# A pipelined attention step in a different order: output and value products moved between two phases of the scores

## The reference

```python
q = split_heads(xn @ Wq (+ bq)); k = split_heads(src @ Wk (+ bk)); v = split_heads(src @ Wv (+ bv))
attn = softmax(q @ k.T * scale (+ mask or relative bias))     # L3_xattn has no softmax
x = x + merge_heads(attn @ v) @ Wo (+ bo)                     # L1_xattn has no Wo; L1/L3_xattn norm afterwards
```

## Time and profile before

| | |
|---|---|
| median of 3 runs | 4896.71 us (4893.21 to 4901.27) |
| the profiled execution | 4900.09 us |
| its span, first to last instruction | 4898.2 us |
| TensorE busy | 4007.7 us, 82% |
| VectorE busy | 3203.4 us, 65% |
| GpSimd busy | 2994.6 us, 61% |
| ScalarE busy | 2059.5 us, 42% |
| mean granted TensorE clock | 0.889 |
| chains run about | 0 to 660, 1240 to 2040, 2300 to 2940, 3680 to 4690 us |

### The profile page before, as it was taken

How to read it: one execution, slowest core, us unless ns; L and a number is a source line. 1 busy time by engine, 2 the same in 40 slices (tenths; PEclk the granted TensorE clock), 3 DMA queues, 4 the chain that set the end, 5 groups by cost and what they waited for, 6 DMA issues and landing times. The chain is left out here.

```text
span 4898.2 us, 215645 instructions
## 1 busy us (share of the span) xinstructions
PE 4007.7 (82%) x85067; PEld 2918.6 (60%) x85076; DVE 3203.4 (65%) x10848; ACT 2059.5 (42%) x5737; POOL 2994.6 (61%) x4949
## 2 busy tenths in 40 slices
PE   8999977254899978656999997559879998889988
PEld 6777754132566666523777774335547776667766
DVE  5875668422344688787556874753337878888866
ACT  4555545011344444365555554112225543336632
POOL 6766632276455699688556762038876777777710
PEclk9999988555899998755999997879998999999999
DMA  3000012433100022200000002113431000000000
GB/s 94 5 13 19 19 28 57 78 62 54 37 0 0 18 39 39 35 1 1 2 0 15 22 18 54 42 46 75 77 62 35 0 15 16 16 9 1 0 13 24
DMA packets 380509, 139.58 MB, mean 28 GB/s; under 512 B 216487, under 2 KB 373239, under 8 KB 380055
## 3 DMA queue, kind: packets, MB, share of 16 engines
q1 hardware_dynamic: 345430, 107.60, 9.3%
q0 software_dynamic: 34816, 28.34, 4.0%
HBM read 91.46 MB, written 43.85 MB: 28 GB/s over the span
## 5 line engine op out<-in xcount | busy, mean ns | idle before, releaser
L1051 DVE TENSOR_REDUCE rowmax<-ps 128x16 f32<-128x1024 f32 x512 | 626.3, 1223 | 488.0 <-PE ps L678 487.7
L696 PE MATMUL ps<-prob,kT 32*64 32x256 f32 x9216 | 781.7, 408 | 8.7 <-issue 2.4
L721 PE MATMUL ps<-v,probT 64*64 64x64 f32 x36864 | 764.6, 227 | 5.3 <-issue 2.2
L721 PEld LDWEIGHTS ps<-v,probT 64*64 64x64 f32 x36864 | 683.8, 140 | 57.4 <-issue 16.0
L678 PE MATMUL ps<-kblock,qT 32*64 32x256 f32 x8192 | 697.0, 410 | 17.2 <-DVE rowmax L1060 14.2
L900 ACT ACTIVATE probT<-ps 128x1024 f32<-128x1024 f32 x512 | 518.0, 1012 | 353.4 <-PE ps L708 353.0
L585 POOL TENSOR_TENSOR kblock<-kT,key_scale 128x512 f32<-128x512 f32 x576 | 599.8, 1041 | 18.2 <-ACT kT L878 7.6
L587 POOL TENSOR_TENSOR prob<-qT,key_scale 128x512 f32<-128x512 f32 x576 | 601.5, 1044 | 0.0
L561 POOL TENSOR_TENSOR vareps<-moments,eps 128x1 f32<-128x1 f32 x522 | 98.8, 189 | 745.7 <-DVE negmean L1025 745.6
L887 ACT ACTIVATE xn<-x_res,nmr,rstd 128x128 f32 (+1 forms) x512 | 252.7, 494 | 513.6 <-POOL nmr L567 349.5
L708 PEld LDWEIGHTS ps<-mT,pick_bf 32*64 32x64 bf16 x16384 | 311.7, 108 | 221.2 <-ACT mT L857 74.1
(11 more groups left out here) (380 smaller groups left out, 9655.7 us busy)
## 6 DMA issues: line engine op xcount, KB each, us to landing
ctxT<-in_ctxT SPq DMA_DIRECT2D x256, 64.0 KB, 1.8
held<-in_g_w SPq DMA_DIRECT2D x16, 836.0 KB
ctxT<-in_ctxT SPq DMA_DIRECT2D x256, 32.0 KB, 1.9
table<-prob SPq DMA_DIRECT2D x32, 256.0 KB, 2.4
x_dram<-x_res SPq DMA_DIRECT2D x32, 256.0 KB, 2.4
x_res<-x_dram SPq DMA_DIRECT2D x16, 512.0 KB, 6.9
x_res<-in_x SPq DMA_DIRECT2D x8, 512.0 KB, 7.5
x_res<-in_e_w SPq DMA_DIRECT2D x64, 64.0 KB
```

The costliest lines, as they stand in the source:

```text
L696: mm = nc.tensor.matmul(out.rearrange("p (h s) -> p h s", h=GH), k.kT[rows, buf, S * b:S * b + S], k.qblock[rows, buf, :, S * b:S * b + S] ...
L721: mm = nc.tensor.matmul(k.ps_o[S * b:S * b + S, u, S * hh:S * hh + S], k.probT[rows, buf, at:at + S], k.v9[rows, buf, (HD + 1) * h:(HD + 1 ...
L1051: nc.vector.tensor_reduce(spread, heads, AX.X, ALU.max).then_inc(soft.did["max_raw"], 1)
```

## The change

TensorE's step starts with the q and k products. Then follow the transposition of xn, the waits of the scores (`scores_writable`, which now asks for `max_raw` and no longer for `max_done`), the transposition of the maxima, mask rows, scores phase one; then the wait for Exp of the tile to be mixed, output product, values, transposition of o; then scores phase two, with the maxima subtracted ahead of the key scores; and last the mix.

ScalarE handles the front (mT, xnT, q, k) first, then oT and v. DVE takes the maximum of the scores ahead of the mix scaling, and its two remainders behind it. The value product is one of 128 columns again (L1_xattn keeps two), and the exchange of the sequences is made by the copy or bias add out of PSUM, in three pieces. The extra columns of xnT and their copy go.

```diff
+def value_parts():
+    first, second, low, high = slice(0, HEADS // 2), slice(HEADS // 2, HEADS), slice(0, S), slice(S, P)
+    return [(slice(0, P), first, slice(0, P)), (low, second, high), (high, second, low)]
...
-        if value is not None or turn is not None or out is not None:
-            after(pe, c, values_read(c, it, 4), it, 4)
-            after(pe, c, "y_read", it, 9)
-            after(pe, c, "oT_done", it, 8)
-        if out is not None:
-            mm = nc.tensor.matmul(k.ps_y, k.oT[:, b8, :], weights(out, 3), start=True, stop=True)
...
+        if mixes is not None:
+            after(pe, c, "v_done", it, mb)
         after(pe, c, "kT_done", it, 3)
...
-            after(pe, c, "max_done", it, 4)
+            after(pe, c, "max_raw", it, 4)
             after(pe, c, "kblock_done", it, 3)
...
         if less is not None:
-            values_mixable(mixes, it, mb)
-            if early:
-                scores_writable(score1, score2, it)
+            scores_writable(score1, score2, it)
             after(pe, c, "max_done", it, 5)
...
-        if mixes is not None:
-            for hh in range(HEADS // 2):
-                mm = mix(mixes, (par - mb) % NB, hh)
-            mm.then_inc(mixes.did["o_psum"], 1)
...
             mm.then_inc(score2.did["first_rows"], 1)
 
+        mm = None
+        if mixes is not None:
+            after(pe, c, "exp_done", it, mb)
+        if value is not None or turn is not None or out is not None:
+            after(pe, c, values_read(c, it, 4), it, 4)
+            after(pe, c, "y_read", it, 9)
+            after(pe, c, "oT_done", it, 8)
+        if out is not None:
+            mm = nc.tensor.matmul(k.ps_y, k.oT[:, b8, :], weights(out, 3), start=True, stop=True)
...
+                mm = nc.tensor.matmul(k.ps_v, source[:, 0:P], wv, start=True, stop=True)
+        if turn is not None:
+            after(pe, c, "on_done", it, 7)
+            mm = nc.tensor.transpose(k.ps_oT, k.o[:, b7, :], k.ident)
+        if mm is not None:
+            mm.then_inc(c.yv_psum, 1)
+
         if score1 is not None:
             after(pe, c, "low_rows", it, 3)
             query_scores(score1, b3, high).then_inc(score1.did["s1_psum"], 1)
...
-            mm = key_scores(score2, b5, low, first=False)
             if less is not None:
                 for h in range(GH):
-                    mm = less_max(less, b5, h, low)
+                    less_max(less, b5, h, low)
+            mm = key_scores(score2, b5, low, first=False)
             mm.then_inc(score2.did["s2_psum"], 1)
+
+        if mixes is not None:
+            for hh in range(HEADS // 2):
+                mm = mix(mixes, (par - mb) % NB, hh)
+            mm.then_inc(mixes.did["o_psum"], 1)
...
-                nc.vector.tensor_tensor(values(k, b3), heads_of(k.ps_v), heads_of(bias),
-                                        ALU.add).then_inc(value.did["v_done"], 1)
+                for rows, heads, source in value_parts() if value.softmax else [WHOLE]:
+                    mm = nc.vector.tensor_tensor(values(k, b3)[rows, heads, :], heads_of(k.ps_v)[source, heads, :],
+                                                 heads_of(bias)[source, heads, :], ALU.add)
+                mm.then_inc(value.did["v_done"], 1)
...
-        k.xnT = sb("xnT", [P, NB, P + S])
+        k.xnT = sb("xnT", [P, NB, P])
```

More of the change, by code:

```diff
@@ L698, in key_scores @@
                     k.qblock[rows, buf, :, S * b:S * b + S],
-                    start=not part.softmax or first, stop=not part.softmax, tile_position=place)
+                    start=not part.softmax or first, stop=not part.softmax or groups == low, tile_position=place)
         return mm
@@ L709, in less_max @@
                     out[:, S * h:S * h + S], k.pick_bf[rows, S * h:S * h + S], k.mT[rows, buf, S * b:S * b + S],
-                    start=False, stop=groups == low and h == GH - 1, tile_position=place)
+                    start=False, stop=False, tile_position=place)
         return mm
@@ L818, in step @@
             mm.then_inc(score2.did["first_rows"], 1)
+        mm = None
[7 more added lines that the diff above has]
+            mm = nc.tensor.matmul(k.ps_y, k.oT[:, b8, :], weights(out, 3), start=True, stop=True)
+        if mixes is not None and turn is None:
+            after(pe, c, "on_done", it, mb + 1)
+        if value is not None:
+            source, wv = k.ctxT[:, b3, :] if value.cross else k.xnT[:, b3, :], weights(value, 2)
+            if value.name == "L1_xattn":
+                nc.tensor.matmul(k.ps_v[:, 0:S], source[:, 0:P], wv[:, 0:S], start=True, stop=True)
+                mm = nc.tensor.matmul(k.ps_v[:, S:P], source[:, S:S + P], wv[:, S:P], start=True, stop=True)
+            else:
+                mm = nc.tensor.matmul(k.ps_v, source[:, 0:P], wv, start=True, stop=True)
[4 more added lines that the diff above has]
+            mm.then_inc(c.yv_psum, 1)
         if score1 is not None:
@@ L842, in step @@
         plain = plain if plain is not None and plain.name == "L3_xattn" else None
[L843 to L847, removed]
-            nc.scalar.activation(k.oT[:, b7, :], k.ps_oT, ACT.Copy).then_inc(turn.did["oT_done"], 1)
-        if value is not None and value.name not in VALUE_BIAS:
-            act.wait_ge(c.yv_psum, it - 2)
-            after(act, c, "y_read", it, 8)
-            after(act, c, "o_psum", it, 3 + NB)
-            nc.scalar.activation(values(k, b3), heads_of(k.ps_v), ACT.Copy).then_inc(value.did["v_done"], 1)
         if norm is not None or project is not None or soft is not None:
@@ L864, in step @@
             else:
-                if not norm.cross:
-                    nc.scalar.activation(k.xnT[:, b1, P:P + S], k.ps_xT[:, 0:S], ACT.Copy)
                 nc.scalar.activation(k.xnT[:, b1, 0:P], k.ps_xT, ACT.Copy).then_inc(norm.did["xT_done"], 1)
@@ L878, in step @@
                 nc.scalar.activation(k.kT[:, b2, :], k.ps_k, ACT.Copy).then_inc(project.did["kT_done"], 1)
+        if turn is not None:
+            act.wait_ge(c.yv_psum, it - 2)
+            after(act, c, "y_read", it, 8)
+            if c.name(it, 3) in VALUE_BIAS:
+                after(act, c, values_read(c, it, 3), it, 3)
+            nc.scalar.activation(k.oT[:, b7, :], k.ps_oT, ACT.Copy).then_inc(turn.did["oT_done"], 1)
+        if value is not None and value.name not in VALUE_BIAS:
+            act.wait_ge(c.yv_psum, it - 2)
+            after(act, c, "y_read", it, 8)
+            after(act, c, "o_psum", it, 3 + NB)
+            for rows, heads, source in value_parts():
+                mm = nc.scalar.activation(values(k, b3)[rows, heads, :], heads_of(k.ps_v)[source, heads, :], ACT.Copy)
+            mm.then_inc(value.did["v_done"], 1)
         if plain is not None:
```

54 lines of the change are left out of this document (17 added, 37 removed).

## The result

The changed kernel takes 5691.2 us (median of 4 runs, 5689.5 to 5702.8) against 4895.2 us before: 1.163 times as long, with an interval of 1.161 to 1.165. It is slower by 796 us. I had forecast 5475 us, slower by 578, with a range to 5680; the measured time is 11 us above its end. The direction and the place were right; three of the sizes were not: the hand-overs from engine to engine, the pieces of the value add, and what the clock takes.

What follows compares the result with a forecast made beforehand. A chain over several engines, not TensorE's work, was taken as the bound, closing in one step after the change. 4900.1 + 483 (loops) + 95 (clock) = 5478, less 3.4 for the runs' median: 5475 us, range 5160 to 5680.

Steps and rivals of the forecast that it cites:

- The ring: Residual add, xn, Exp, phase one, products, transposition, back to the add: closes in one step, 5.44 us against 4.56 in L0_attn.
- The hand-overs: Signals between engines in the loop: Exp's end to weight load 0.05 us; transposition 0.28 plus 0.06 to DVE's add.
- The value pieces: DVE's value bias add cut in three, in L0_xattn, L1_attn, L3_attn: 0.22 us extra, between none and 0.58.
- The sum of the rings: Step increases of the seven attention stages, together 7.54 us, times 64 tiles: 483 us.
- The clock: TensorE's waits lower its granted clock in seven stages to near L1_xattn's 0.91: 95 us, near ends 0 and 130.
- the clock falls deep: Rival: two gaps in every step, longer with a bias, bring the granted clock to 0.70; 5810 us, 10%.
- L1_xattn and L3_xattn: Stages forecast unchanged: DVE and GpSimd fill L1_xattn, DVE's own loop covers L3_xattn; up to 32 us if that cover fails.
- A shorter loop binds: Rival: if Exp is not last, the loop through GpSimd's kblock binds at 4.92 us a step; 5200 us, 13%.
- The clock stays up: Rival: the same loop without the 95 us for the clock; 5380 us, 22%.
- The loop does not close: Rival: TensorE's own work sets the step, 4.1 us, with masks 4.64 and 5.97; 4659 us, faster; 6%.
- The wait of L708: TensorE's stall for the maxima's transposed copy, 0.35 us in L0_attn before the change, was to vanish.

Runs made afterwards that it cites:

- adding the mix to the ring: Kernel before, with output product, values and transposition between the score phases and ScalarE's front ahead of oT and v; mix left ahead of phase one: 6855.9 us.
- the kernel with the products added: Changed kernel with useless repeats of the q and k products on TensorE while it waits for xn and Exp: 5529.8 us, ratio 1.130.
- the two runs with added products: Useless q and k products added to the changed kernel (5529.8 us), and in L1_xattn alone to the kernel with DVE's and ScalarE's queues reordered (4684.5 us).
- the run with the moments first: Changed kernel with DVE's moments of the next tile ahead of the residual and value adds and L3_xattn's sums: 4884.6 us, ratio 0.998.
- the first experiment: Changed kernel with Exp ahead of xn in ScalarE's step instead of behind it: 5270.3 us, ratio 1.076.
- the last kernels: Changed kernel with DVE's moments ahead of its adds, ScalarE's xn and Exp ahead of oT and v: 4692.8 us; with whole values 4749.3; useless L1_xattn products 4684.5.

## Why the prediction was right and where it was wrong

**The ring: right.** The prediction said that output, values and transposition, once behind the wait for Exp, close a chain in one step that had needed two. Four runs bear it out from four sides: cutting the ring at DVE, cutting it at Exp, moving the block back to the head, and adding the mix to the ring, with 4885, 5270, 4877 and 6856 us. Most of the pieces read from L0_attn held too. From the residual add to xn 2.19 us came for 2.18, xn to Exp 0.40 for 0.40, phase one 0.74 for 0.75, output and value products 0.55 for 0.56.

**The hand-overs: too small.** This is the first step that failed. Exp's end to TensorE's weight load was read as 0.05 us from the earlier trace rows and is 0.18 in the step shown; the transposition's start to DVE's add was put at 0.34 and is 0.42. With 0.01 elsewhere that ring is 5.66 and not 5.44 us. As means over 42 rounds of L0_attn in the kernel with the products added, where the clock is 1.00, the two are 0.21 and 0.46: 0.28 us more than priced, and 0.28 x 448 = 125 us. Of the first, 0.10 is the two waits that TensorE's queue reads after Exp's; the run with their order changed shows it. Why the second is longer stays open.

**The value pieces: too small.** I took 0.22 us for two more pieces, "nearer to the low end since each piece is small". They cost 0.52, near the high end of the range that I had written down (0.58). 0.30 x 3 x 64 = 58 us. This was a choice between two ends, made by the amount of data, and the cost did not go by it.

**The sum of the rings.** Forecast 483, measured 635 at full clock: 152 us missing. In the middle of the stages the forecast was short by more than that. The column with the products added stands 0.30 to 0.31 us above it in the four stages without a value bias and 0.59 to 0.61 in the three with one, together 3.0 us, or some 190 us over 64 tiles. The two terms above give 183 of these. At a stage's ends the steps are shorter, though, and the seven stages as wholes lost 608 us, some 65 less than 64 middle tiles each would have; the other 26 were lost in L1_xattn and L3_xattn, which were forecast at nothing. That the total is short by only 152 is in part luck.

**The clock: too small.** Forecast 95, measured 161, 66 us missing. The way was right, the level was not. I had read 0.91 and 0.96 off L1_xattn and L3_xattn, and the stages with a bias or two sets of moments went to 0.85 to 0.87. The prediction's own rival "the clock falls deep" had named the stages with a bias as those with the longer gaps, and priced 0.70 for all. Among the seven stages the order is as that rival has it: TensorE stands still 1.1 to 1.2 us a step at 0.97 to 0.99, and 1.4 to 1.9 at 0.85 to 0.87. But the prediction's inference from idle time to clock does not carry over to other stages: L1_xattn, with 1.0 us a step, has 0.81, and L0_xattn with the products added, with 1.2, has 1.00. So no run here gives a way by which 0.85 could have been worked out. In L1_attn alone the clock takes 1.35 us a tile, half of all that it takes.

**L1_xattn and L3_xattn: nearly right.** They were put at no change and rose by 0.23 and 0.12 us a tile. For L1_xattn the two runs with added products show that it was the clock (6.04 us at 0.99), and so that a stage can be slowed by an engine that isn't its bound. The mean clock is not the whole of it, since the kernel before has the same 6.04 us at 0.91. L3_xattn was put down to DVE's own loop; the run with the moments first, at 5.13 us with the same instructions, shows that DVE's order and not its work made that loop as long as 6.16.

**The rivals.** "A shorter loop binds" was not what happened, but it is what the first experiment uncovered, 0.20 us above its price; the same hand-overs are missing in it. "The clock stays up" was wrong. "The loop does not close" needed DVE's and ScalarE's queues in another order, which the last kernels have: 4.34 us a tile against the 4.1 that I had summed for TensorE's own work, and 4.77 and 6.07 against 4.64 and 5.97.

The wait of L708 (L717 after) for the maxima's copy was to vanish. It shrank, from 0.35 to 0.20 us of idle weight loads. Phase one still takes 0.74 us, so what is left lies under its products and costs the ring nothing.

## What to carry to other kernels

In a software pipeline over engines, count for every chain how many steps it takes to come back to its start; the time of a step is the chain divided by that number. Moving a block past a wait can turn two steps into one without a single instruction getting longer, and the cure may be in the queue of an engine that is half idle: look for work of the next tile queued behind a wait that belongs to another tile. When a term lies on such a ring, price it by the number of instructions and of waits and not by the amount of data, take each hand-over as a mean over many steps, and leave room for what TensorE's clock takes from its part.

## What was not expected of the hardware

- In this kernel a semaphore wait on TensorE's queue is not free even when its signal has come: two of them read after the decisive one cost 0.06 us in most steps and 0.10 on the mean, and ordering them ahead gave 45 us in all.
- An add of 64 columns on 128 or on 64 partitions, out of PSUM with a bias, takes 0.23 to 0.25 us from start to start on DVE, where one of 128 columns takes 0.20. Here half and quarter the data saved nothing.
- The granted clock is not told by how long TensorE stands still. At 1.0 to 1.2 us a step it was 0.81 (L1_xattn), 0.97 (L0_attn) and 0.99 (L2_attn) in the changed kernel, and 1.00 (L0_xattn) with products added. What it costs can be large: L1_attn takes 8.35 us a tile at 1.00 and 9.70 at 0.85. Some 0.7 us of useless products a step, all in idle time, gave back 161 us in the changed kernel.
